# A graph layer's one-hot sums in units of seven chunks instead of four, and a first stage unrolled with its statistics one round ahead

## What is computed

```python
edge_index = jnp.stack([src, dst])
x = x + gcn(layernorm(x), ...)        # h = x @ W1 (512 -> 8); degree-weighted sums over edges; W2 (8 -> 512)
x = x + ffn(layernorm(x), ...)        # ternary weights, 512 -> 1408 -> 512
x = x + mean_conv(layernorm(x), ...)  # agg = segment_sum(xn[src], dst); agg / max(deg, 1); x + alpha * (agg @ W.T + b)
x = x + switch_moe(layernorm(x), ...) # 16 experts
```

## Time and profile before

| what | value |
|---|---|
| median of the runs | 3950.85 us |
| profiled execution, its own time | 3950.55 us |
| span of its trace | 3948.8 us |
| busy in the span: PE, DVE, ACT, POOL | 71%, 53%, 27%, 53% |
| first stage | 0 to about 301 us |
| fourth stage: first gather, first visit, last gather | 2417.7, 2451.8, 3561.2 us |
| time outside the span | 1.75 us |

### The profile page before, as it was taken

One profiled execution on the slowest core, in us unless ns is written; L12 is line 12 of the kernel. 1 busy time (PEld: TensorE's weight loads), 2 busy tenths in 40 slices (PEclk: granted clock), 3 DMA queues, 4 the chain that ended last, 5 costly groups with the idle time before them and its releaser, 6 DMA issues. The chain is left out here.

```text
span 3948.8 us, 60722 instructions
## 1 busy us (share of the span) xinstructions
PE 2807.3 (71%) x16139; PEld 2048.0 (52%) x16140; DVE 2086.5 (53%) x3745; ACT 1053.4 (27%) x1677; POOL 2087.1 (53%) x2184
## 2 busy tenths in 40 slices
PE   3664556320399999999999994677666676766599
PEld 3564555320277777777777883223232232323487
DVE  7777888992345454545454434443434434343476
ACT  1234446200123232323232331011111121213344
POOL 0006777775777777777500003776656665660254
PEclk9998778655599999999999997999999999997699
DMA  1113224102023333333322324777666666762464
GB/s 53 48 39 59 53 46 110 15 5 37 4 65 108 84 100 84 102 82 106 83 97 83 101 89 149 221 234 215 191 205 201 201 206 184 220 196 81 141 212 132
DMA packets 249317, 458.11 MB, mean 116 GB/s; under 512 B 93442, under 2 KB 115058, under 8 KB 249094
## 3 DMA queue, kind: packets, MB, share of 16 engines
q0 software_dynamic: 112384, 235.97, 23.1%
q1 hardware_dynamic: 136710, 219.40, 17.3%
HBM read 388.49 MB, written 73.25 MB: 117 GB/s over the span
## 5 line engine op out<-in xcount | busy, mean ns | idle before, releaser
L1611 POOL DMA_INDIRECT rows<-xn_rows,srcT x784 | 741.1, 945 | 403.6 <-issue 216.3
L115 POOL DMA_INDIRECT msg_c<-hid_rows,srcT x784 | 758.2, 967 | 251.2 <-issue 232.8
L1711 PE MATMUL pV<-rows,oh 128*128 x1952 | 474.1, 387 | 241.2 <-DVE agg L1872 193.8
L115 POOL DMA_INDIRECT msg_b<-hid_rows,srcT x464 | 455.7, 982 | 148.5 <-issue 137.2
L1711 PEld LDWEIGHTS pV<-rows,oh 128*128 x1952 | 190.6, 98 | 511.5 <-issue 356.9
L1273 PE MATMUL acc<-wd,hT 128*128 128x512 f32 x1617 | 414.8, 405 | 3.1 <-issue 1.2
L1248 PE MATMUL pG<-xT,wgu_hi 128*128 128x512 f32 (+1 forms) x1232 | 371.1, 382 | 22.9 <-issue 21.3
L1248 PE MATMUL pU<-xT,wgu_hi 128*128 128x512 f32 (+1 forms) x1232 | 364.2, 377 | 13.2 <-DVE sil L1417 13.2
L1884 DVE SCALAR_TENSOR_TENSOR oh<-ids,bases,dstT 128x512 f32 x244 | 183.2, 751 | 357.0 <-issue 322.7
L1273 PEld LDWEIGHTS acc<-wd,hT 128*128 128x128 f32 x1617 | 306.9, 193 | 77.4 <-issue 13.8
L1872 DVE TENSOR_TENSOR agg<-agg,pV x245 | 167.8, 685 | 269.2 <-PE pV L1711 257.8
(11 more groups left out here) (362 smaller groups left out, 4625.9 us busy)
## 6 DMA issues: line engine op xcount, KB each, us to landing
wd<-wd_rows SPq DMA_DIRECT2D x154, 512.0 KB
we<-in_L_ffn_expert_w SPq DMA_DIRECT2D x16, 1024.0 KB, 8.0
msg_c<-hid_rows,srcT POOLq DMA_INDIRECT x784
x_rows<-xr SPq DMA_DIRECT2D x49, 256.0 KB, 4.1
xn_rows<-pair SPq DMA_DIRECT2D x49, 256.0 KB
rows<-xn_rows,srcT POOLq DMA_INDIRECT x784
res<-x_rows SPq DMA_DIRECT2D x49, 256.0 KB, 3.9
x_rows<-agg SPq DMA_DIRECT2D x49, 256.0 KB, 2.9
```

The costliest lines, as they stand in the source:

```text
L115: nc.gpsimd.indirect_dma_start(msg[:, c, :], None, table, bass.IndirectOffsetOnAxis(ap=srcT[:, c:c + 1], axis=0)).then_inc(landed[u % 2], 16)
L1611: nc.gpsimd.indirect_dma_start(rows[:, u % RING, c, :], None, xn2_rows, bass.IndirectOffsetOnAxis(ap=srcT[:, u * Q + c:u * Q + c + 1], axi ...
L1711: last = nc.tensor.matmul(pV[:, ds(to, 1), :].rearrange("p a d -> p (a d)"), oh[:, ds(of, 1), c, :].rearrange("p a d -> p (a d)"), rows[:, ...
```

## The change

Fourth stage: Q goes from 4 to 7 and RING from 7 to 4, so that the ring holds 28 chunks as before; there are 112 units for 196. The one-hot buffers go from four to two, and VectorE's separate wait for them is dropped, since the wait in `add_pending` of the visit before covers it. GpSimd asks for a unit's landing after the fourth DMA of the next unit, with two semaphores in turn in place of four. The second stage computes the table of units with a multiplication and a shift by 16 in place of a shift by 2.

First stage: the lists are loaded in 96, 15 and 1 partitions, the 96 before anything is cleared; `w1` is loaded after the first seven tiles of x; the loops of all four engines are written out. The statistics of round i+1 are spread over the histogram units of round i; x, its statistics and scales and the hidden product have two buffers, the histogram's one-hots four. The list turns are four of up to 512 columns; two of them, the tile extremes, spans and table rows move into round 0, the low bytes into round 1. TensorE's order in a round is histogram m, turn m, layer1 m-1.

```diff
-Q = 4
+Q = 7
-RING = 7
+RING = 4
-AHEAD = 3
+LANDING = 4
...
+                EA = 96
+                for lst, em, done in lists:
+                    sp.dma_start(em[0:EA, :], lst[0:EA * EB * P].rearrange("(p c) -> p c", p=EA)).then_inc(s[done], 16)
                 sp.wait_ge(s["cleared"], 2)
-                for lst, em, done in ((src, src_em, "src_in"), (dst, dst_em, "dst_in")):
-                    sp.dma_start(em[0:EP - 1, :], lst[0:full].rearrange("(p c) -> p c", p=EP - 1)).then_inc(s[done], 16)
+                for lst, em, done in lists:
+                    sp.dma_start(em[EA:EP - 1, :], lst[EA * EB * P:full].rearrange("(p c) -> p c", p=EP - 1 - EA)).then_inc(s[done], 16)
                     sp.dma_start(em[EP - 1:EP, 0:E - full], lst[full:E].rearrange("(p c) -> p c", p=1)).then_inc(s[done], 16)
...
+                first = {1: extreme_tiles, 2: lambda: turned_list(2), 3: lambda: turned_list(3), 4: spans, 6: span_rows, 7: tile_ranges}
...
+                statistics(0, range(G))
+                variance(0)
+                for i in range(G):
+                    for m in range(HG):
                         histogram(i, m)
+                        if i == 0 and m == 0:
+                            scales(0)
+                        if i == 0 and m in first:
+                            first[m]()
+                        if i == 1 and m == 0:
+                            low_ids()
+                        if i + 1 < G:
+                            if m < 4:
+                                statistics(i + 1, range(2 * m, min(2 * m + 2, G)))
+                            if m == 4:
+                                variance(i + 1)
+                            if m == 6:
+                                scales(i + 1)
...
+                for i in range(G):
+                    for m in range(HG):
                         histogram(i, m)
+                        if i == 0 and m in first:
+                            first[m]()
+                        if m < G:
+                            turn(i, m)
+                        if m > 0:
+                            layer1(i, m - 1)
...
                 def arrived(u):
-                    pool.wait_ge(landed[u % (AHEAD + 1)], (u // (AHEAD + 1) + 1) * Q * 16)
+                    pool.wait_ge(landed[u % 2], (u // 2 + 1) * Q * 16)
                     pool.sem_inc(s["rows_ready"], 1)
...
-                    if u >= AHEAD:
-                        arrived(u - AHEAD)
-                for u in range(CQ - AHEAD, CQ):
-                    arrived(u)
+                        if c + 1 == LANDING and u > 0:
+                            arrived(u - 1)
+                arrived(CQ - 1)
...
-            oh = sb(ctx, "oh3", [P, 4, Q, P], F16)
+            oh = sb(ctx, "oh3", [P, 2, Q, P], F16)
...
-                            wait_alone(dve, s["mm_done"], v + 1, s["fence_dve"])
                             nc.vector.scalar_tensor_tensor(
-                                oh[:, ds(v % 4, 1)].rearrange("p a q n -> p (a q) n"), bc(ids.unsqueeze(1), (P, Q, P)), bases[:, ds(tile, 1)],
+                                oh[:, ds(v % 2, 1)].rearrange("p a q n -> p (a q) n"), bc(ids.unsqueeze(1), (P, Q, P)), bases[:, ds(tile, 1)],
```

More of the change, by code:

```diff
@@ L36 @@
 assert all(n * BY_U >> 16 == n // U for n in range(C + 2 * U))
-Q = 4
+Q = 7
 CQ = C // Q
+BY_Q = -(-(1 << 16) // Q)
+assert CQ * Q == C and all(n * BY_Q >> 16 == n // Q for n in range(C))
 M = 80
@@ L432, in _ @@
                 for k in range(G):
                     load(0, k)
-                with sp.Fori(1, G - 1) as i:
+                sp.dma_start(w1[:], W1.rearrange("(k p) h -> p k h", p=P)).then_inc(s["w1_in"], 16)
+                for i in range(1, G):
                     for k in range(G):
-                        sp.wait_ge(s["xT_ps"], (i - 1) * G + (k + 1))
                         load(i, k)
-                for k in range(G):
-                    sp.wait_ge(s["xT_ps"], (G - 2) * G + k + 1)
-                    load(G - 1, k, P if k < G - 1 else LAST)
@@ L476, in _, with statistics @@
                 own = Steps(dve, s["dve"])
-                nc.vector.memset(src_em[:], 0).then_inc(s["cleared"], 1)
-                nc.vector.memset(dst_em[:], FAR).then_inc(s["cleared"], 1)
-                dve.wait_ge(s["dst_in"], 32)
+                def statistics(i, ks):
+                    for k in ks:
+                        dve.wait_ge(x_in[i % 2][k], (i // 2 + 1) * 16)
+                        last = nc.vector.bn_stats(st[:, k, :], xt[:, i % 2, k, :])
+                    own.step(last)
@@ new lines, in variance, with scales @@
+                def variance(i):
+                    if i >= 2:
+                        dve.wait_ge(s["xn"], (i - 1) * G)
+                    for k in range(G):
+                        last = nc.vector.bn_aggr(mv[:, i % 2, k, :], st[:, k, :])
+                    own.step(last)
+                    own.step(nc.vector.tensor_scalar_add(var[:, i % 2], mv[:, i % 2, :, 1], EPS))
+                    dve.sem_inc(s["var"], 1)
+                def scales(i):
+                    dve.wait_ge(s["std"], i + 1)
+                    newton(nc, own, rs[:, i % 2, :, 0], var[:, i % 2], nw[:])
+                    nc.vector.scalar_tensor_tensor(rs[:, i % 2, :, 1], mv[:, i % 2, :, 0], -1.0, rs[:, i % 2, :, 0],
+                                                   ALU.mult, ALU.mult).then_inc(s["stats"], 1)
@@ L493, in _ @@
-                own.step(nc.vector.tensor_tensor(pres[:, 1], bc(mm[:, 1, :].unsqueeze(2), full), tiles, ALU.is_ge))
-                own.step(nc.vector.tensor_tensor(pres[:, 2], pres[:, 0], pres[:, 1], ALU.mult))
-                for j in range(2):
-                    own.step(nc.vector.tensor_tensor(pres[:, 0], pres[:, 2], bc(cid[:, j, :].unsqueeze(2), full), ALU.mult))
-                    own.step(nc.vector.tensor_reduce(span[:, j, :], pres[:, 0].rearrange("p e t -> p t e"), AX, ALU.max))
-                nc.vector.tensor_copy(pres[:, 1, 0, 0:1], pres[:, 0, 0, 0:1]).then_inc(s["span"], 1)
@@ L510, in _ @@
                 own.step(nc.vector.tensor_copy(lo_f[:], lohi_i[:, 1, :]))
-                nc.vector.tensor_copy(hiT_f[:], lohi_i[:, 2, :]).then_inc(s["lo_hi"], 1)
-                dve.wait_ge(s["span_ps"], 1)
-                nc.vector.tensor_reduce(spanr[:], pL[0][0:2 * NT, 0:EP], AX, ALU.max).then_inc(s["spanr"], 1)
-                dve.wait_ge(s["row_ps"], 1)
-                r = [row[0:1, j, :] for j in range(8)]
-                own.step(nc.vector.tensor_copy(row[0:1, 0:2, :].rearrange("p a b -> p (a b)"), pL[1][0:1, 0:2 * NT]))
@@ L579, in _ @@
                 dve.sem_inc(s["hid1"], 1)
+                own.step(nc.vector.tensor_scalar_max(invdeg[:], pD[:, 0:NT], 1.0))
+                own.step(nc.vector.reciprocal(invdeg[:], invdeg[:]))
                 own.step(nc.vector.tensor_mul(degroot[:], degs[:], dinv[:]))
@@ new lines, in turn_list, with spans @@
+                    last.then_inc(s["lists_ps"], 1)
+                for j in range(4):
+                    turn_list(j) if j < 2 else None
+                nc.tensor.matmul(pD[:, 0:NT], identb[:], zeros[:], start=True, stop=False)
+                def spans():
+                    pe.wait_ge(s["span"], 1)
+                    pe.wait_ge(s["lists_used"], 4)
+                    nc.tensor.transpose(pL[0][0:2 * NT, 0:EP], span[:].rearrange("p a b -> p (a b)"),
+                                        ident[0:EP, 0:EP]).then_inc(s["span_ps"], 1)
```

268 lines of the change are left out of this document (139 added, 129 removed).

## The result

The changed kernel takes 3738.36 us, median of 4 runs (3730.91 to 3743.15), for 3950.85 before (also 4 runs, 3946.94 to 3951.02): a ratio of 0.9463, 95% interval 0.9446 to 0.9480. The profiled execution took 3737.77 us, its span is 3736.1. The forecast was 3751 in a range of 3720 to 3825.

A forecast was written before the change was run, and what follows sets the result against it. No engine full in the first stage; in the fourth, TensorE's sequencer sets visits, POOL's gathers close behind. Profiled 3950.55 less 68 (first stage) and 132 (fourth: 115 plus 17) gives 3750.6, forecast 3751, within 3730 to 3775; wider range 3720 to 3825.

The forecast's parts named there:

- Lists: First stage: 96 partitions go to 16 engines, so the first conversion starts at 5.6 us, between 4.5 and 9, for 18.72.
- VectorE's sum in the first stage: First stage: from the first conversion VectorE's work alone sums to 218.9 us, ending at 224.5 where it ended at 293.5.
- The last round: First stage's last round, without statistics: TensorE and VectorE are equal there, costed at 2 us.
- Visits: Fourth stage, TensorE: sequencer time sets visits of 14 pairs, 4.5 us apart at a unit's end and 3.1 within.
- The later tiles: Fourth stage, sums of tiles 15 to 48: 34 tiles gain 3.39 us each, 115 us.
- The start: Fourth stage's early tiles, paced by POOL: turned sums of tile 13 at 2741 for 2758.15, a gain of 17 us.
- 221 x 1.25: Fourth stage's start: POOL's gathers after the 29th at 2456.6, 1.25 us each, bring the announcement of unit 34 to 2733.
- POOL's margin: Fourth stage: POOL alone could reach the last gather at 3400 against 3429, 29 us to spare, ring waits about 54 us.
- Array and sequencer in series: Rival 1, fourth stage: array and overhead follow each other in a visit, gain 85 us for 132, 3798; chance 0.13.
- POOL's coarser ring: Rival 2, fourth stage: the coarser ring binds POOL and costs 20 to 60 us, 3770 to 3810; chance 0.2.
- Landing: Rival 4, fourth stage: POOL stalls at the landing question, slower than before, 4030 or so at 9 us; chance 0.03.
- Part of the first stage not coming: Rival 3: lists late (+13) or VectorE still waiting every round (+21), 3764 to 3785; chance 0.12.

The follow-up runs named there:

- the half columns: Third-sum matmuls 256 of 512 columns wide, in the kernel before (3982.80 us, ratio 1.0083) and in the changed kernel (3740.15 us, ratio 0.9462).
- a ring of three: Changed kernel with `RING = 3` in place of 4 (21 chunks for 28): 3820.06 us, ratio 0.9667.
- the run with two: Changed kernel with `LANDING = 2` in place of 4, asking for a unit's landing after two gathers: 3831.02 us, ratio 0.9697.
- first stage only: Kernel before with only the first stage's part of the change: 3872.27 us for 3952.52, ratio 0.9801.
- lists only: Kernel before with only the list loads changed (96, 15 and 1 partitions, the 96 ahead of the clears): 3936.11 us, ratio 0.9965.
- half columns before: Kernel before with each matmul of the third sum 256 instead of 512 columns wide: 3982.80 us, ratio 1.0083.
- the run with two histogram buffers: Changed kernel with `HB = 2` in place of 4 in the first stage: 3736.40 us, ratio 0.9463.
- the question after five: Changed kernel announcing a unit five gathers after its last in place of four: 5545.51 us (ratio 0.9688) on the slow chip, 3739.40 us (0.9463) on a usual one.

## Why the prediction was right, point by point

The bound before the change, the place of both gains and their sizes were right: 212.5 us measured by the medians, 200 forecast. The forecast is 13 us high, of which 14 us lie in stages to which it gave nothing, 3 in the fourth, and the first took 5 back. That it is no further off is in part luck, as the fourth stage shows below.

**Lists.** First conversion forecast at 5.6 us, measured 6.12. Right.

**VectorE's sum in the first stage.** Forecast 218.9 us from there, measured 220.7 (6.12 to 226.85, the end of the last one-hots). Right within 1%. In it a smaller part was missed: the two copies of the target list (L511) take 3.19 us together, where the seven small ones took 3.7, so that merging them saved 0.5 us; the forecast had dropped the small ones and put nothing in their place. The four buffers, which it named as cover, are not needed.

**The last round.** Forecast 2 us for TensorE, measured 4.47. This term was mis-sized. The reckoning took "equal" from a sum per round. But a unit, a turn and a layer take TensorE 3.02 us and VectorE's unit 2.72, so it falls behind by 0.3 us a unit: its last unit starts at 228.81, 1.96 us after VectorE's last one-hots end, and one more layer stands between it and the closing matmul (229.38 to 231.08). Closing `pD` before that last layer would take up to 1.7 us off, an estimate; that was not tried.

**Visits.** Forecast 4.46 to 4.5 us at a unit's end and 3.1 within. Measured 3.09 within, in 36 of 48; at a unit's end 4.4 to 4.5 is the commonest value, but only in 16 of 111. The split of a visit into 0.14 us a pair and a fixed part held when the pairs went from 8 to 14 (2.24 to 3.09 us within a unit) and when the array's time was halved. It failed at the low clock, where the forecast had said that nothing shows 14 pairs queued: 4.4 to 4.7 us, set by the array. It cost little only because these visits fell into tiles that POOL bounds. The Trainium skill, "TensorE: Matmul & The Clock Gate", section "Architectural detail: the array is 16x 32x32, not 1x 128x128", gives TensorE's queue room for 64 instructions, and the 28 of a visit are fewer; that at the full clock they came every 3.09 us with and without half the array's work agrees with it. No run here shows the 64.

**The later tiles.** Forecast 34 tiles by 3.39 us, 115; measured 125.3 over 35 tiles (844.1 of the earlier trace rows less 718.8), 3.58 each; why it is 0.19 more a tile stays open. That TensorE and not POOL sets these tiles held: it waits for no announcement in them. **The start.** Forecast 17 us; measured 7.7: tile 13's turned sums are 332.7 us after the first gather for 340.5. Two things were off. "Nothing moves that" of the 29th gather: it comes 40.8 us after the first for 38.9, since its wait for a slot is 6.04 us for 4.16. And "221 x 1.25" leaves out two stops of POOL, 9.4 us beyond the usual gap. The 29th gather and the two stops:

```profile
2384.57 0.95 POOL L1663 DMA_INDIRECT rows<-xn_rows,srcT  x1 [6.04 <-DVEq L1940]
...
2495.89 0.94 POOL L1663 DMA_INDIRECT rows<-xn_rows,srcT  x1 [5.16 <-issue]
...
2640.74 0.94 POOL L1663 DMA_INDIRECT rows<-xn_rows,srcT  x1 [4.87 <-issue]
```

The errors of the two terms, 10 us up and 9 down, cancel: 133.0 us for 132. That is luck.

**POOL's margin.** The forecast gave POOL 29 us to spare and 54 us of slot waits. Slot waits are 22.2 us in nine; this term was too large, as the stops that no term had took 23.9 of POOL's time. First to last gather is 1027.6 us; 979.5 are gathers at their usual distance, 23.9 are six stops with no releaser, 20.8 the other gaps, which stand at a unit's end or its landing question, and the rest is gathers that took longer than usual. So POOL went through its own stream in all but some 21 us, and the stage can give at most that as long as POOL issues the gathers and makes these stops. The last gather is at 3371.4 for the 3361 forecast.

**The rivals.** Array and sequencer in series: refuted by the half columns at the full clock, true of 14 pairs at the low clock. POOL's coarser ring: it did not cost 20 to 60 us with four units, and its sign, TensorE waiting for POOL in the later tiles, isn't there; but the mechanism is real, and a ring of three shows that sign and costs 82. Landing: the forecast of none was right with the question after four gathers, and the rival's price for a wait on POOL (in full, once its slack is used) is what the run with two shows. Both rivals were sound mechanisms a step away from this change, and 7 chunks a unit with four slots lies just inside them. Part of the first stage not coming: 5 of 68 us.

**Third stage.** 9.3 us that no term had. The likeliest cause is the place of TensorE's code, above, though no run shows the 9.3 us by themselves. It couldn't be foreseen from the profile before; that the loop's end costs 5 us a round could be seen in it.

## What to carry to other kernels

Where the profile names a consumer as the releaser but the visits keep their distance at the low clock, cost the sequencer per pair and per loop end; it then scales to other unit sizes, but cost the array at the low clock beside it, since with more pairs it can overtake. When an engine's own stream fills the new time of a stage to 98%, a wait on it costs in full once the last 2% are used: size rings and questions with one step to spare, and test one step less to see it. Total waits don't tell who is late; the time from an announcement to the consumer's start does. Before acting on a wait in a table, divide it by its count, and compare the quotient with the gap that the engine has anyway.

## What the runs showed of the hardware

- **With units of seven, POOL stops every 112 gathers.** In the fourth stage of the changed kernel gaps of 3.4 to 5.2 us with no releaser stand before the gathers number 114, 226, 338, 450, 562 and 674 (counted from 1), 23.9 us beyond the usual gap, and at the same numbers (3.2 to 5.5 us) in every kernel with units of seven on the usual chips. In those with units of four (before, first stage only, lists only, half columns before) the gaps at these numbers are the usual 0.30. So these stops came with the change and took 24 us of POOL's time, 9.4 of them in the tiles whose pace POOL sets. On the slow chip named below, where the gather before had waited 5 to 12 us for a slot, they are 0.64. What the number 112 stands for wasn't tried.
- **Narrower matmuls lower the clock.** 256 columns in place of 512, with the same instructions at the same distance, took the stage's mean granted clock from 0.95 to 0.70.
- **The clock decides which side sets a visit of 14 pairs.** At the full clock a visit of 14 pairs is 3.09 us with 512 columns and with 256. At the low clock it is 3.1 with 256 and, depending on how much of it is at that clock, up to 4.7 with 512 (granted 0.64; 5.8 at 0.52 in the run with two histogram buffers).
- **Where code lies changes the stops at a loop's end**: 1.9 to 2.3 us for 4.9 to 5.6, with only TensorE's earlier code longer (the two traces are from different chips).
- **In one set of runs the kernel before took 45% longer.** There the second stage of the changed kernel with the question after five (249.7 to 1803.7) took 1554 us for 752 at the same count of instructions. In it and in the first feed-forward round TensorE's instructions came 2.8 us apart, with nothing that the profile shows between:

```profile
1867.80 0.58 PE L1300 MATMUL pG<-xT,wgu_lo 128*128 128x512 f32 x1 [2.22 <-issue]
1870.60 0.59 PE L1300 MATMUL pG<-xT,wgu_hi 128*128 128x512 f32 x1 [2.22 <-issue]
```

The first stage there took as long as elsewhere (second stage's gathers from 249.7), and so did the later feed-forward rounds (191.0 to 191.2 us), which have no gathers beside them, and the fifth stage (253.3 for 252.5). The slow stretch begins when the second stage's gathers start and ends soon after those beside the third stage do (2492). The fourth stage, again with gathers beside it, is slow again: 1363.4 us from first to last gather for 1023.7, with POOL's gathers at their usual 1.25 us and 379.1 us of waits for slots. So TensorE or VectorE was late there, not POOL. Why it is so stays open. The record gives these runs the same chip number, 2, as the ring of three, beside which the kernel before took 3949.51 us, so it may be a state of the chip and not the chip.
